# Recurrence on 28 segments of 112 steps in place of 16 segments of 196, with the table of tokens stored in whole chunks

## What is computed

```
t = t + linear_attention(layernorm(t))          # cumulative sums over T
def _L1_ffn_ref(x, W, V, gamma, beta):           # called with layernorm(t)
    Wx = einsum('bti,hi->bth', x, W)
    Wx = (Wx - mean) * rsqrt(var + eps) * gamma + beta     # mean, var over all B*T tokens
    def step(yt, wx_t):
        yt = sigmoid(wx_t + yt @ V.T)
        return yt, yt
    _, ys = scan(step, zeros(B, H), Wx over T)   # T steps, one after the other
t = t + ys
```

## Time and profile before

| what | us |
|---|---|
| three runs | 1784.03, 1787.8, 1788.23 (median 1787.8) |
| the profiled execution, its own time | 1784.76 |
| its span, first to last instruction | 1782.8 |
| of it the recurrence, first matmul 1574.56 to the end of the last 1773.4 | 198.8 |
| what stands behind that matmul | 9.4 |
| PE, DVE, ACT, POOL busy | 1749.7, 1509.8, 1269.8, 1073.7 |

### The profile page before, as it was taken

How to read it: one execution, slowest core, us unless ns; L and a number is a source line. 1 busy time by engine, 2 the same in 40 slices (tenths; PEclk the granted TensorE clock), 3 DMA queues, 4 the chain that set the end, 5 groups by cost and what they waited for, 6 DMA issues and landing times.

```text
span 1782.8 us, 58142 instructions
## 1 busy us (share of the span) xinstructions
PE 1749.7 (98%) x19648; PEld 1587.7 (89%) x19648; DVE 1509.8 (85%) x4546; ACT 1269.8 (71%) x3387; POOL 1073.7 (60%) x1202
## 2 busy tenths in 40 slices
PE   7999999999999999989999999999999999989997
PEld 6888888888888888879999999999999999989997
DVE  7889888888888888778888888888888888868787
ACT  5877778887887788856666666666666666657776
POOL 6887888888888888843333333333333333368874
PEclk9999999999999999999999999999999999999999
DMA  5333343433333332313334434343434443457774
GB/s 167 105 103 104 104 110 99 109 107 102 110 103 104 106 106 70 83 43 70 73 67 68 70 68 70 68 67 68 70 68 70 68 68 70 86 178 277 291 278 176
DMA packets 361816, 188.30 MB, mean 106 GB/s; under 512 B 221760, under 2 KB 348720, under 8 KB 356656
## 3 DMA queue, kind: packets, MB, share of 16 engines
q1 hardware_dynamic: 360368, 183.40, 41.0%
q10 hardware_dynamic: 1152, 1.13, 0.2%
HBM read 106.58 MB, written 77.87 MB: 103 GB/s over the span
## 4 chain that ended last, share of the span: by engine, by line
PE 52%; issue 28%; POOL 17%; DVE 1%; DMA 1%; POOLq 0%; ACT 0%; ACTq 0%; SPq 0%; DVEq 0%
POOL la_rstd L1025 12%; PE k_psum L349 7%; PE k_psum L299 6%; PE k_psum L292 6%; PE k_psum L1488 6%; PE k_psum L317 6%; PE k_psum L333 6%; PE k_psum L365 5%; PE k_psum L1478 5%; PE k_psum L283 5%; POOL la_spread L1019 3%; POOL la_tn L1030 2%; DMA wa_group<-in_group 0%; POOLq L42 0%; DMA t<-la_tn 0%
## 5 line engine op out<-in xcount | busy, mean ns | idle before, releaser
L1019 POOL TENSOR_SCALAR la_spread<-la_mv 128x4 f32<-128x4 f32 (+1 forms) x203 | 46.2, 228 | 476.1 <-DVE la_mv L1130 476.0
L618 POOL TENSOR_TENSOR wa_prob<-wa_prob,wa_peak 128x784 f32<-128x784 f32 x128 | 195.0, 1523 | 116.8 <-DVE wa_peak L484 116.8
L966 ACT ACTIVATE la_ve<-k_psum 128x256 f32<-128x256 f32 x196 | 75.6, 386 | 231.9 <-PE k_psum L847 231.9
L1025 POOL TENSOR_TENSOR la_rstd<-la_spread,k_exponent 128x4 f32<-128x4 f32 (+1 forms) x203 | 207.8, 1024 | 17.2 <-POOL la_spread L1019 0.4
L625 POOL TENSOR_TENSOR wa_prob<-wa_prob,wa_inv 128x784 f32<-128x784 f32 x128 | 195.2, 1525 | 11.3 <-DVE wa_inv L445 11.3
L835 PE MATMUL k_psum<-la_uT,la_wt 128*128 128x256 f32 x784 | 201.9, 380 | 0.0
L1085 DVE SCALAR_TENSOR_TENSOR la_fqk<-k_psum,la_raised 128x512 f32<-128x512 f32 x196 | 135.4, 691 | 72.8 <-ACT la_raised L958 72.6
L1562 ACT ACTIVATE sc_y<-k_psum,sc_cols 128x128 f32<-128x128 f32 x414 | 152.3, 368 | 51.9 <-PE k_psum L1488 8.8
L476 DVE TENSOR_TENSOR wa_prob<-k_psum,wa_bias 128x784 f32<-128x784 f32 x128 | 124.9, 976 | 66.2 <-PE k_psum L317 66.1
L1488 PE MATMUL k_psum<-sc_y,sc_vT 128*128 128x128 f32 x824 | 171.0, 289 | 0.0
L958 ACT ACTIVATE la_raised<-k_psum,la_minus_one 128x512 f32<-128x512 f32 x196 | 134.8, 688 | 43.9 <-PE k_psum L835 43.7
(11 more groups left out here) (137 smaller groups left out, 5205.3 us busy)
## 6 DMA issues: line engine op xcount, KB each, us to landing
la_xc<-x SPq DMA_DIRECT2D x196, 128.0 KB, 3.0
wa_xT<-in_x_cm SPq DMA_DIRECT2D x124, 196.0 KB, 3.3
sc_tb<-t SPq DMA_DIRECT2D x17, 1320.0 KB, 8.3
out<-sc_ob SPq DMA_DIRECT2D x17, 1280.0 KB, 5.4
wa_xw<-in_x_tok SPq DMA_DIRECT2D x64, 224.0 KB, 2.7
wa_xw<-in_x_tok SPq DMA_DIRECT2D x64, 168.0 KB, 2.3
x<-wa_y SPq DMA_DIRECT2D x64, 168.0 KB, 2.8
x<-wa_y SPq DMA_DIRECT2D x48, 224.0 KB, 2.9
```

The lines of the kernel that those rows point to most:

```text
L618: nc.gpsimd.tensor_tensor(s, s, peak[:, k % S, :].unsqueeze(2).broadcast_to([128, PAIRS * HEADS, WIN]), ALU.subtract).then_inc(lowered, 1)
L1025: nc.gpsimd.tensor_tensor(rstd[:, n % S, used], spread[:, used], exponent[:, used], ALU.pow).then_inc(rooted, 1)
```

## The change

`SEGS` becomes 28, so `STEPS` = 112, `COLS` = 448, `HALF` = 224, and the table has 14 blocks in place of 8. With 12 warm steps the recurrence has 124 steps in place of 208. A tile has at most 6 steps in place of 10 (`LONGEST`), the main table is 2, 4, 16 times 6, 5, 3, 2. DVE works on single steps of 448 elements a row, four steps ahead of the states; POOL takes 4 steps of a tile's 6. The rings of `uT` and `y` are 5 steps each (they were 4 and 3 pairs). `EARLY_BLOCKS` is 12 of 14, which puts `EARLY_AT` to unit 182. A chunk of 128 tokens is stored by one DMA, whatever segments it touches. The core of the diff:

```diff
-SEGS = 16
+SEGS = 28
...
-        def pieces(n):
...
+        def table_rows(c):
+
+            first, block = c * P, SQ * STEPS
+            return bass.AP(t2.tensor, (first % block * NB + first // block) * SF, [[NB * SF, P], [block * NB * SF, QUADS], [1, SF]])
...
-                    for a, p, q, col, s in pieces(n):
-                        dst = bass.AP(t2.tensor, ((col % SQ * STEPS + s) * NB + col // SQ) * SF,
-                                      [[NB * SF, q - p], [SQ * STEPS * NB * SF, QUADS], [1, SF]])
-                        sp.dma_start(dst, tn[p:q, n % XS, a]).then_inc(stored[n % XS], 16)
+                    for a in range(2):
+                        sp.dma_start(table_rows(2 * n + a), tn[:, n % XS, a]).then_inc(stored[n % XS], 16)
...
-MAIN_PLAN = [(0, 4, True), (4, 8, True)] + [(12 + 10 * j, 10, True) for j in range(17)] + [(182, 8, True), (190, 4, True), (194, 2, True)]
+MAIN_PLAN = [(0, 2, True), (2, 4, True)] + [(6 + 6 * j, 6, True) for j in range(16)] + [(102, 5, True), (107, 3, True), (110, 2, True)]
...
-LONGEST = 10
+LONGEST = 6
 KEPT_TILES = 3
-U_PAIRS = 4
-Y_PAIRS = 3
-EARLY_BLOCKS = 7
+U_STEPS = 5
+Y_STEPS = 5
+EARLY_BLOCKS = 12
...
-        return plan[j][1] // 2 * 3 // 5 if FIRST <= j < TILES - 2 else 0
+        return plan[j][1] * 2 // 3 if FIRST <= j < TILES - 2 else 0
...
-        def turn_tokens(p):
-            if not inside(p, PAIRS):
+        def turn_tokens(t):
+            if not inside(t, NT):
                 return
-            j, i = where[p]
+            j, i = where[t]
             dve.wait_ge(u_made, j + 1)
-            at_least(dve, w_done, 4 * (p - U_PAIRS + 1))
-            nc.vector.transpose(uT[:, p % U_PAIRS].rearrange("p s c -> p (s c)"),
-                                ub[:, j % 2, i:i + 2].rearrange("p s b r -> p (s b r)")).then_inc(u_turned, 1)
+            at_least(dve, w_done, 2 * (t - U_STEPS + 1))
+            nc.vector.transpose(uT[:, t % U_STEPS, :], ub[:, j % 2, i].rearrange("p b r -> p (b r)")).then_inc(u_turned, 1)
...
-        for p in range(-3, PAIRS + 1):
-            hand(p)
-            turn_states(p - 1)
-            if p == PAIRS:
+        for t in range(-4, NT + 1):
+            hand(t)
+            turn_states(t - 1)
+            if t == NT:
...
-            turn_tokens(p + 3)
-            residual(p - 1)
+            turn_tokens(t + 4)
+            residual(t - 1)
```

More of the change, by code:

```diff
@@ L723, in quads @@
             return tile.rearrange("p (q r) -> p q r", q=QUADS)
-        def pieces(n):
[L727 to L735, removed]
+        def table_rows(c):
+            first, block = c * P, SQ * STEPS
+            return bass.AP(t2.tensor, (first % block * NB + first // block) * SF, [[NB * SF, P], [block * NB * SF, QUADS], [1, SF]])
         def stores_through(k, units):
-            return 16 * sum(len(pieces(m)) for m in range(k, units, XS))
+            return 32 * len(range(k, units, XS))
         def quotient_bank(n):
@@ L1247, in state @@
     def state(self, t):
-        return self.tiles["y"][:, t // 2 % Y_PAIRS, t % 2, :]
+        return self.tiles["y"][:, t % Y_STEPS, :]
     def sum_weights(self, pe, sums):
@@ L1385, in scan @@
     TILES = len(plan)
-    where = [(j, i) for j in range(TILES) for i in range(0, plan[j][1], 2)]
-    PAIRS = len(where)
-    NT = 2 * PAIRS
+    where = [(j, i) for j in range(TILES) for i in range(plan[j][1])]
+    NT = len(where)
     FIRST = sum(not kept for _, _, kept in plan)
-    pairs_to = [sum(size for _, size, _ in plan[0:j]) // 2 for j in range(TILES + 1)]
-    WARM_PAIRS = pairs_to[FIRST]
-    WARMED = 2 * WARM_PAIRS
+    steps_to = [sum(size for _, size, _ in plan[0:j]) for j in range(TILES + 1)]
+    WARMED = steps_to[FIRST]
     def by_pool(j):
-        return plan[j][1] // 2 * 3 // 5 if FIRST <= j < TILES - 2 else 0
+        return plan[j][1] * 2 // 3 if FIRST <= j < TILES - 2 else 0
     def loads(j):
@@ L1410, in vector_sums, with vector_steps @@
     def vector_sums(j):
-        return sum(plan[i][1] // 2 - by_pool(i) for i in range(FIRST, j))
+        return sum(plan[i][1] - by_pool(i) for i in range(FIRST, j))
+    def vector_steps(t):
+        return sum(i >= by_pool(j) for j, i in where[WARMED:max(WARMED, t)])
     def slot(j):
@@ L1475, in input_part @@
                 pe.wait_ge(ffn.ready, 1)
-            pe.wait_ge(u_turned, t // 2 + 1)
+            pe.wait_ge(u_turned, t + 1)
             at_least(pe, y_made[h], t - 1)
-            nc.tensor.matmul(b_state[h][t % 2][:, 0:HALF], ffn.fT[:, :], uT[:, t // 2 % U_PAIRS, t % 2, half(h)],
+            nc.tensor.matmul(b_state[h][t % 2][:, 0:HALF], ffn.fT[:, :], uT[:, t % U_STEPS, half(h)],
                              start=True, stop=False).then_inc(w_done, 1)
@@ L1512, in hand, with turn_states @@
             nc.vector.memset(begins[:, :, 0:1], 0.0).then_inc(handed, 1)
-        def turn_states(p):
-            if not inside(p, PAIRS) or p < WARM_PAIRS:
+        def turn_states(t):
+            if not inside(t, NT) or t < WARMED:
                 return
-            j, i = where[p]
+            j, i = where[t]
             for h in range(2):
-                dve.wait_ge(y_made[h], 2 * p + 2)
+                dve.wait_ge(y_made[h], t + 1)
             at_least(dve, stored[slot(j)], stores(j))
-            states = y[:, p % Y_PAIRS].rearrange("p s c -> p (s c)")
-            if i < 2 * by_pool(j):
-                nc.vector.transpose(ob[:, slot(j), i:i + 2, :].rearrange("p s c -> p (s c)"), states).then_inc(y_turned, 1)
-            else:
-                nc.vector.transpose(b_y[p % 2], states).then_inc(y_turned, 1)
@@ L1527, in residual @@
-        def residual(p):
-            if not inside(p, PAIRS) or p < WARM_PAIRS:
+            if i < by_pool(j):
+                nc.vector.transpose(ob[:, slot(j), i, :], ffn.state(t)).then_inc(y_turned, 1)
+            else:
+                at_least(dve, summed, vector_steps(t - 1))
+                nc.vector.transpose(b_y[t % 2][:, 0:COLS], ffn.state(t)).then_inc(y_turned, 1)
+        def residual(t):
+            if not inside(t, NT) or t < WARMED:
                 return
-            j, i = where[p]
-            if i < 2 * by_pool(j):
+            j, i = where[t]
+            if i < by_pool(j):
```

23 lines of the change are left out of this document (11 added, 12 removed).

## The result

| | before | after |
|---|---|---|
| median of 18 runs each, same chip, us | 1784.89 | 1790.53 |
| lowest to highest | 1782.45 to 1788.98 | 1787.2 to 1792.03 |
| the profiled execution, its span | 1782.8 | 1789.6 |
| first to last matmul of the recurrence | 198.8 | 190.8 |
| last unit's factor to the first matmul | 8.6 | 14.9 |

The ratio is 1.0030, interval 1.0023 to 1.0037: slower by 0.3% (5.6 us), at the edge of what was called no change. The forecast was 1782.8 us: a sum of -3.4 us, laid on 1786.2, the mean of the four times known then. The recurrence gained more than forecast; two terms beside it were far off.

A forecast was written before the change was run, and what follows sets the result against it. PE was taken to bound the kernel, busy nearly all the span, 94% filled in the recurrence. Terms -6.7 - 0.4 + 2.0 + 1.0 + 0.7 = -3.4 us, laid on 1786.2, gave 1782.8 us, range 1776 to 1791.

The forecast's parts named there:

- The recurrence: 124 steps of 1.53 us, set by PE's own work, in place of 208 of 0.947: -6.7 us, bounds -8.0 and +0.2.
- the mild form of the loop: Rival in the recurrence: loads landing after 10.2 us make a tile 9.55 us, +5.9, 1788.7 us; chance 0.04.
- the gap that stays: Rival in the recurrence: the odd 0.05 us a step belongs to semaphores and stays, +6.8, 1789.6 us; chance 0.07.
- The loop of POOL and loads: Rival in the recurrence: POOL's work and load landings set the tile from 9.5 us landing on, 1788.7 to 1799 us; chance 0.17.
- The early loads: Ahead of a load of tokens on SP's queue: 2.43 MB in place of 1.42 delay it, +2.0 us, bounds 0 and +2.8.
- The hand-over: Last unit to first step of the recurrence: one store issue fewer, -0.4 us, bounds -1.2 and +0.3.
- The early scaling: POOL's two early multiplications take 4.4 us in place of 2.58 and stall DVE: +1.0 us, bounds 0 and +1.7.
- Behind the recurrence: After the last step: four DVE instructions on 432 elements in place of 240, +0.7 us, bounds 0.3 and 1.2.

The follow-up runs named there:

- e4: The change with EARLY_BLOCKS 7 in place of 12, early loads 1.42 MB in place of 2.43, at unit 112; 1781.43 us, one time (kernel before 1782.93).
- e7: e1 with its table padded from 8 to 14 blocks a step, tokens 1848 bytes apart; 1792.62 us, one time (kernel before 1783.23).
- e2: The change, 28 segments, but with the old stores, cut where a segment ends; 1786.76 us, ratio 1.0025 to the kernel before.
- the repeated run: The change itself, unchanged, profiled a second time; 1788.98 us, one time (kernel before 1783.23).
- e1: The kernel before, 16 segments and old table, with each chunk of 128 tokens stored by one DMA; 1781.32 us, ratio 0.9992 to the kernel before.
- e3: The change with its three early loads issued from ACT's queue in place of SP's; 1780.6 us, ratio 0.9992 to the kernel before.
- e8: The change with early loads in six parts, one per unit, and only one tile scaled early; 1776.19 us, ratio 0.9967 to the kernel before.
- e14: e8 again, the same kernel measured a second time; 1779.01 us, ratio 0.9976 to the kernel before.
- e9: e8 with the chunks of the last three units stored in halves of 64 rows; 1779.93 us, ratio 0.9978 to the kernel before.

## Why the prediction was wrong

The measured 1790.53 us lies inside the forecast range, 1776 to 1791, and that is luck. The upper end was drawn for two things that didn't occur, the mild form of the loop and the gap that stays. The sum of the terms was -3.4 us and the difference of the medians is +5.6.

**The recurrence: the mechanism was right, the term too small.** Predicted -6.7, measured -8.0. A matmul was put at 0.3825, "a little high", and measured 0.378, what the line between the two rows gave; over 124 x 4 of them that is 2.1 us. In the other direction the start at 1.2 GHz costs more: eight matmuls took 5.95 us in place of 3.02, 2.9 us, against 1.7 before (twelve from 1574.56 to 1578.94, of 128 columns, 4.38 in place of 2.67). The low clock already stands at the first matmul in the change, after the longer wait for the hand-over; I had carried the old start over. The rival in which the odd 0.05 us stays is refuted: no third distance, and ACT waits for PE, not PE for ACT.

**The loop of POOL and loads** didn't close. It decides from a landing of 9.5 us, and the median is 8.5, below the 8.8 that I forecast; POOL's spare time of 0.8 us a tile is as forecast, and the few late loads (6.7 us in five waits) are taken up by it and by tokens turned four steps ahead.

**The early loads are the first step that failed.** The term was +2.0, "nearer to the bytes", with bounds of 0 and +2.8; +9.3 came. The rate was right: up to 1512 some 390 GB/s are moved. What failed is the upper bound, which held only if all else at the burst costs what it cost before. Three things broke that. The added bytes delayed the load behind them by more than their own time, 4.9 us in place of 2.8 (7.7 us to landing in e4, 12.6 in the change). The new table and stores added 1.2 us with no byte more (6.5 to 7.7 us); e7 shows that a placing can add more (1.9 to 5.5 us of wait), and with cut stores the load lands after 10.4 us in place of 12.6 (e2). And behind this wait the granted clock fell: PE was idle for 7.0 us and then ran at half speed for 5, which costs 2.4 more and had no term. In e4 PE waited 1.5 us behind its early loads and its clock stayed at 1.00. A view of before held the warning, that the microseconds before 1528.88 moved little:

```profile
1527.00:1528.00 1.00, 1.00 (x11) 0.92 (x10) 0.00 (x0) 0.82 (x3) 0.68 (x2) 1.00 1.07 256
1528.00:1529.00 1.00, 1.00 (x12) 1.00 (x11) 0.12 (x1) 0.80 (x3) 0.00 (x0) 1.00 0.43 47
```

I used that as an argument for a lower term, though it said that a load can be late with few bytes to blame.

**The hand-over is the second.** It read -0.4, "with two chunks one issue goes", bounds -1.2 and +0.3; +6.3 came (4 in the repeated run). The count of issues was right in its sign, as e2 shows. The landing of the last store was taken from a piece on the old table, with the argument that bigger, evener stores can only help. They don't on this table: whole chunks close together land in 6.2 to 10.1 us in every kernel that has them with 28 segments and in 7.7 in e7, in 4.2 on the old table, and in 2.75 and 3.24 where the last units' chunks are cut. The slow landing needs both parts of the change, whole chunks and a new placing, and I had priced each part as if the other weren't there. With 28 segments the cut stores are no way out either: e2 loses as much to its ten issues. That the table's placing had changed at all, with 1848 bytes between a chunk's tokens in place of 1056, stood in the diff and got no term and no bound.

**The early scaling** was right in its mechanism and low in size: +1.6 for +1.0. The stall lasts until POOL ends, 2.62 us where 1.22 was the longest before; I took 0.66 us of PE's slack off it, but the stall grew by 1.4 and 1.6 were lost, so no slack came off. The Trainium skill ("SBUF — State Buffer", the section on its two sides and ports) has VectorE and GpSimd hold their shared ports exclusively, and by that rule the stall had to grow with the multiplication, as it did.

**Behind the recurrence** +0.9 for +0.7.

The slower outcome had a chance of 0.13, all of it by the loop, which didn't occur. It came by a way for which no rival stood.

**What stays open.** Which property of the table's placing makes bunched stores slow; what the last store waits for in its last 4 us, in which almost nothing is moved; its spread, 7.7 and 10.1 us in one kernel; why the clock falls near 767 us in some executions and not in others. Why the added bytes delay the load behind them by more than their own time wasn't separated further: e4's burst also stands at another unit, at 1223 us.

## What to carry to other kernels

A block of loads that is put ahead of one that an engine needs is priced by when that one lands, and a wait after which PE's clock falls costs more than itself: 7.0 us became about 10 here. Cut the block into one part per unit, which lost only 0.65 to 1.5 us here and gave back 0.56%. When a table in HBM changes shape, its stores and loads get a term with a wide upper bound, even if bytes and counts are the same: here the shape alone took a last store from 4.2 to 7.7 us. A change of two parts is to be priced as a pair too. Whole chunks were harmless on the old table, and 28 segments landed cut stores fast; each part's price for the last store changed with the other.

## What was unexpected of the hardware

- 128 rows of 4 x 132 bytes a DMA: where such stores stand close together on the new table, the DMA share reads 1.6 to 1.8 with 37 to 56 GB/s moved (1575 to 1579 in the change); on the old one it is 0.54 to 0.67 with 67 to 100 GB/s (cut stores before, whole ones in e1).
- A 128 KB load behind a burst of 2.43 MB landed after 12.6 us, and in the last two microseconds of it 80 GB/s were moved at a DMA share of 0.95.
- After 7 us of idle time PE's granted clock was 0.50 for some 5 us of work; after 2.6 us (e3) it was so too, after 1.5 us (e4) it wasn't. A matmul of 224 float32 columns took 0.75 us at this level and 0.378 at 2.4 GHz.
- Near 767 us the granted clock fell to 0.50 for some 3 us in some executions and not in others, with the same waits of PE before it, also in two executions of one kernel (e8, e14). It is worth 1.3 us.
- Issues of stores on SP's queue took 0.43 to 0.70 us each when several stood in a row, a single one up to 2.00 (e9), so four halves cost about as much as they saved.
